# Making the one-hots of an edge sort column by column with scalars per partition, and loading the destinations first

## The chip, the cores and the metric

One core of a Trainium2 chip runs the kernel. Its engines are TensorE (PE), VectorE (DVE), ScalarE (ACT), GpSimd (POOL) and SyncE (SP); each works off its own list of instructions in order and waits on semaphores for the others. The metric is the device time of one execution in microseconds; less is better.

## What is computed

Four layers of a graph network on 1250 nodes with 512 features and 21250 edges (20000 random ones in both directions and a loop at each node, ordered by destination): an attention layer with batch normalization, an equivariant message layer, an attention layer followed by splines, and a mean aggregation. Each is followed by a residual addition and a layer normalization. Cut to what matters here:

```python
def reference(x, src, dst, edge_attr_4, edge_attr_8, ...):
    edge_index = stack([src, dst])
    x = layernorm(x + gat(x, edge_index, ...))              # per edge: h[src], softmax over dst
    x = layernorm(x + messages(x, edge_attr_4, edge_attr_8, edge_index, ...))
    x = layernorm(x + spline_attention(x, edge_index, ...))
    x = layernorm(x + mean_of_neighbours(x, edge_index, ...))
    return x
```

The kernel turns the edge list into a dense matrix of counts (how many edges lead from each node to each other), with which the attention layers work. For that the edges have to be grouped by blocks of nodes first. This grouping, the sort, is what the change touches.

## The kernel before

**Layout of the edges.** The 21250 edges lie as 125 partitions x 170 columns (`EC` = 170). VectorE computes for each edge the place it has in an order by blocks (40 groups of destinations for the records, then 20 groups for the counts): one-hot masks, a scan along the free dimension, totals over the partitions by TensorE (lines 825 to 831), and from these a place, which is split into a tile (0 to 203) and a lane (0 to 127).

**The sort.** TensorE moves two values per edge, the source `src_f` and the destination within its block `dl1`, to their lane and tile: for each of the 170 columns one matmul with weights [125 edges x 128 lanes], which hold the value at the edge's lane, and moving data [125 edges x 204 tiles], a one-hot of the tile. All accumulate into two PSUM banks. The columns go in 17 rounds (`ROUNDS`) of 10 (`SB`), with buffers for 3 rounds (`SBUFS`). In a round VectorE makes the lane one-hots of ten columns in one `tensor_tensor` (line 1962), the tile one-hots in another (1963), and multiplies the lane one-hots by the source in a third (1965). Their operands are broadcast: `iota2` holds each number twice, and two columns lie interleaved. ScalarE makes the second product, lane one-hot times `dl1`, by one ACTIVATE Copy with a scale per partition for each column (`scale_lanes`, line 1468). TensorE waits for both (835, 839). Between the rounds VectorE clears a fifth of the count matrix in rounds 4 to 8 (1967) and adds the residual identity to `w_skip` in round 10 (1974).

**What runs beside it.** TensorE works off node blocks of the first layer (`gat_block`, line 856) before the rounds and after the fourth and ninth batch; ScalarE copies them out (`gat_out`, 1473). At the end of the rounds stand small products for the attention rows (862, 871) and the group numbers (902 to 929). GpSimd writes the 170 columns of edge records to DRAM, one indirect DMA each (line 728), from the moment that VectorE has their places (1906) until long after the sort; ScalarE reads them back (1555) for an MLP on TensorE (1011 to 1036).

**Behind the sort.** VectorE copies the sorted lists out of PSUM (1987, 1988), makes one-hots of them (1996, 2005), TensorE counts pairs (942), ScalarE evicts (1524), VectorE adds (2015). Then follow the mask (2029), the maxima over neighbours of eight heads (2050) and the attention heads (2080, 2084, 1638, 1090).

**The start.** SyncE issues, in this order, `dst`, `src`, the two edge attributes, the second half of `x` (lines 542 to 549, two DMAs each), then 16 small DMAs of attention vectors, the clearing of the records in DRAM and the small weights. ScalarE's queue begins with the first half of `x` and `w_gat` (1431 to 1433). VectorE's first real work (1859) waits for `dst`. TensorE's list begins with the totals that VectorE's first scan (1865) gives (825), then come the transposes of `x` (849).

Of the kernel before, what the change touches and what calls it, by code (L numbers as in the profile page):

```python
# [12 lines left out]
EC = E // NP  # L13
# [80 lines left out]
def build(nc, a, out):  # L94
# [8 lines left out]
    with ctx:  # L103
# [6 lines left out]
        def sem(name):  # L110
            return ctx.enter_context(nc.semaphore(name))
# [70 lines left out]
        def nxt(shape, dt=f32):  # L182
# [43 lines left out]
        tile_f, lane_f = dstf.bitcast(f16)[:, 0:EC], posf.bitcast(f16)[:, 0:EC]  # L226
        src_f = dstf.bitcast(f16)[:, EC:2 * EC]
# [3 lines left out]
        lane_oh, lane_src, lane_dl = (at(off, [NP, SBUFS * PR, 2 * 128], f16).rearrange("p a (c t) -> p a c t", t=2)  # L231
                                      for off in (9980, 1020, 2940))
        tile_oh = cnt_s[:].rearrange("p b n -> p (b n)")[:, 4 * N:4 * N + SBUFS * PR * 2 * NSORT].bitcast(f16)\
            .rearrange("p (a c t) -> p a c t", a=SBUFS * PR, t=2)
# [174 lines left out]
        s_lane_ok = sem("s_lane_ok")  # L409
        s_lane_cp = sem("s_lane_cp")  # L410
# [128 lines left out]
        def _(sp):  # L539

            x_rows = a["x"].rearrange("(b p) n -> p b n", p=NP)
            for dst_tile, view, done in (
                    (dsti, a["dst"].rearrange("(p e) -> p e", p=NP), s_dst_in),
                    (srci, a["src"].rearrange("(p e) -> p e", p=NP), s_rec_in),
                    (a4, a["edge_attr_4"].rearrange("(p e) k -> p e k", p=NP), s_rec_in),
                    (a8, a["edge_attr_8"].rearrange("(p e) k -> p e k", p=NP), s_rec_in),
                    (x_sb[:, HB:, :], x_rows[:, HB:, :], s_x_in1)):
                for r in ROWS:
                    sp.dma_start(dst_tile[r], view[r]).then_inc(done, 16)
# [264 lines left out]
        def _(pe):  # L814
# [18 lines left out]
            def sort_batch(j):  # L833
                pe.wait_ge(s_sort_ok, j + 1)
                pe.wait_ge(s_lane_cp, j + 1)
                for n in range(SB):
                    r, e = (j % SBUFS) * PR + n // 2, n % 2
                    for q, lane in enumerate((lane_src, lane_dl)):
                        ins = t.matmul(PS[:, q, 0:NSORT], lane[:, r, :, e], tile_oh[:, r, :, e],
                                       start=(j == 0 and n == 0), stop=(j == ROUNDS - 1 and n == SB - 1))  # L840
                ins.then_inc(s_order_ps, 1)
# [586 lines left out]
        def _(act):  # L1428
            A = nc.scalar.activation

            for r in ROWS:
                act.dma_start(x_sb[r, 0:HB, :], a["x"].rearrange("(b p) n -> p b n", p=NP)[r, 0:HB, :]).then_inc(s_x_in, 16)
# [29 lines left out]
            def scale_lanes(j):  # L1462
                act.wait_ge(s_lane_ok, j + 1)
                if j >= SBUFS:
                    act.wait_ge(s_order_ps, 3 + j - SBUFS)
                for n in range(SB):
                    r, e, c = (j % SBUFS) * PR + n // 2, n % 2, j * SB + n
                    ins = A(lane_dl[:, r, :, e], lane_oh[:, r, :, e], ACT.Copy, scale=dl1[:, c:c + 1])  # L1468
                ins.then_inc(s_lane_cp, 1)

            def gat_out(b):
                act.wait_ge(s_h_ps, b + 1)
                A(h_sb[:, b, :], PS[:NP, 6 + b % 2, :], ACT.Copy).then_inc(s_h_cp, 1)
# [30 lines left out]
            for j in range(ROUNDS):  # L1504
                scale_lanes(j)
                if j in (4, 9):
                    gat_out(NB - 2 + j // 9)
                if j == ROUNDS - 3:
                    quad_out(0, 2)
                    quad_out(1, 3)  # L1510
                if j == ROUNDS - 2:
                    quad_out(2, 2)
                if j == ROUNDS - 1:
                    rows_out(0)
                    rows_out(1)
# [332 lines left out]
        def _(dve):  # L1848
# [102 lines left out]
            for j in range(ROUNDS):  # L1951
                if j >= SBUFS:
                    dve.wait_ge(s_order_ps, 3 + j - SBUFS)
                rs = slice((j % SBUFS) * PR, (j % SBUFS + 1) * PR)

                def of_pairs(vals, width):
                    return vals[:, j * SB:(j + 1) * SB].rearrange("p (a t) -> p a t", t=2).unsqueeze(2)\
                        .to_broadcast([NP, PR, width, 2])

                def numbers(width):  # L1960
                    return iota2[:NP, 0:2 * width].rearrange("p (c t) -> p c t", t=2).unsqueeze(1).to_broadcast([NP, PR, width, 2])
                v.tensor_tensor(lane_oh[:, rs], numbers(128), of_pairs(lane_f, 128), ALU.is_equal).then_inc(s_lane_ok, 1)
                v.tensor_tensor(tile_oh[:, rs], numbers(NSORT), of_pairs(tile_f, NSORT), ALU.is_equal)
                dve.wait_ge(s_lane_ok, j + 1)
                v.tensor_tensor(lane_src[:, rs], lane_oh[:, rs], of_pairs(src_f, 128), ALU.mult).then_inc(s_sort_ok, 1)
                if 4 <= j < 9:
                    ins = v.memset(cnt_d[:, (j - 4) * 2 * SPAN:(j - 3) * 2 * SPAN], 0)
                    if j == 8:
                        ins.then_inc(s_const0, 1)
# [573 lines left out]
```

## Time and profile before

| | us |
|---|---|
| median of three runs | 1570.6 (1567.6 to 1571.47) |
| the profiled execution | 1571.28 |
| its span | 1569.8 |
| busy: TensorE, VectorE, ScalarE, GpSimd | 1370.8, 1353.6, 903.3, 479.7 |
| first work on `dst` (VectorE, line 1859) | starts at 8.47 |
| rounds of the sort on VectorE | 70.39 to 135.9 |
| batches of the sort on TensorE | 86.5 to 144.5 |
| sorted lists read by VectorE | from 146.7 |

The profile is of one execution. Times in it count from the start of its span. A line such as L1468 is a line of the kernel. The chain of waits follows the work that ended last back through what released it; a timeline lists instructions in order of time, and neighbours of one line are merged (x50). "idle before" is the time for which the engine stood still ahead of the instruction, with the engine and line that ended it.

### The profile page before, as it was taken

The page shows a single profiled execution, that of the slowest core. Times are in us where ns is not written, and L with a number is a line of the kernel's source. Part 1 is how long each engine was busy: PE and PEld are TensorE (multiplying, and loading weights), DVE is VectorE, ACT ScalarE, POOL GpSimd, SP SyncE. Part 2 cuts the span into 40 slices and gives each one's busy share as a digit, 9 for nine tenths or more (in the row PEclk, how much of TensorE's full clock was granted, in tenths as well). Part 3 has the DMA queues.
Part 4 walks back from the last instruction along what each step waited for, and adds up shares of the span by engine and source line. Part 5 has one row for each costly group of instructions (what it writes and reads, how often), then busy time and mean ns, then how long its engine had stood idle before and what let it go on. Part 6 is the DMA issues. An engine that isn't in the chain of part 4 may idle for free.

```text
span 1569.8 us, 25159 instructions
## 1 busy us (share of the span) xinstructions
PE 1370.8 (87%) x8237; PEld 884.0 (56%) x8237; DVE 1353.6 (86%) x2066; ACT 903.3 (58%) x1949; POOL 479.7 (31%) x488
## 2 busy tenths in 40 slices
PE   2877988738688878689999999978999999999998
PEld 1555444512333333476666666765667777776465
DVE  7965999999899999869999999887989989997244
ACT  1176555718555555568888888642258849772400
POOL 1688888840001101226666666200000000000000
PEclk9799999859699999789999999988999999999999
DMA  8001000026211121247666766500144435333401
GB/s 195 4 6 8 7 7 7 6 79 173 69 56 57 37 72 22 69 131 214 204 197 191 216 201 195 91 1 1 41 147 135 134 121 174 135 134 100 126 20 46
DMA packets 77815, 150.27 MB, mean 96 GB/s; under 512 B 14850, under 2 KB 33396, under 8 KB 77605
## 3 DMA queue, kind: packets, MB, share of 16 engines
q1 hardware_dynamic: 51395, 83.19, 16.5%
q0 software_dynamic: 23328, 59.50, 14.9%
q10 hardware_dynamic: 3010, 6.59, 1.5%
q8 instruction: 38, 0.62, 0.2%
q14 instruction: 44, 0.36, 0.1%
HBM read 116.13 MB, written 32.91 MB: 95 GB/s over the span
## 4 chain that ended last, share of the span: by engine, by line
PE 45%; DVE 29%; issue 16%; ACT 5%; DVEq 3%; DMA 1%; POOL 0%; SPq 0%; POOLq 0%; ACTq 0%
PE PS L1320 14%; DVE arena L2084 7%; DVE arena L2050 5%; PE PS L1272 4%; DVE arena L2246 4%; PE PS L1330 4%; DVE arena L2080 3%; PE PS L1405 3%; PE PS L942 3%; ACT arena L1468 2%; PE PS L1385 2%; PE PS L1395 2%; DVEq L2246 2%; DVE arena L2005 2%; PE PS L1301 1%
## 5 line engine op out<-in xcount | busy, mean ns | idle before, releaser
L728 POOL DMA_INDIRECT recs<-arena x170 | 238.6, 1404 | 90.9 <-issue 90.3
L1090 PE MATMUL PS<-arena 125*128 125x512 f32 (+1 forms) x480 | 190.5, 535 | 41.6 <-DVE arena L2084 41.6
L792 POOL DMA_INDIRECT arena<-xup,gidx x205 | 195.0, 951 | 101.4 <-issue 49.3
L1178 PEld LDWEIGHTS PS<-arena 128*32 128x32 f32 x3280 | 173.1, 109 | 86.4 <-ACT arena L1706 79.8
L1706 ACT ACTIVATE arena<-arena,gslot 128x32 f32<-128x32 f32 x820 | 186.2, 309 | 51.8 <-PE PS L1178 45.4
L1178 PE MATMUL PS<-arena 128*32 128x128 f32 (+1 forms) x3280 | 200.4, 304 | 4.7 <-DVE arena L2238 2.2
L2238 DVE TENSOR_TENSOR arena<-PS,arena 128x1536 f32<-128x1536 f32 (+1 forms) x103 | 179.3, 1740 | 0.0
L1090 PEld LDWEIGHTS PS<-arena 125*128 125x128 f32 x480 | 86.0, 191 | 146.2 <-issue 78.1
L1638 ACT ACTIVATE arena<-arena,c 125x1250 f32<-125x1250 f32 x80 | 106.7, 1336 | 97.3 <-DVE arena L2080 97.2
L1320 PE MATMUL PS<-arena,cnt_d 128*125 128x256 f32 x576 | 147.8, 379 | 0.0
L2080 DVE SCALAR_TENSOR_TENSOR arena<-arena,c 125x1250 f32<-125x1250 f32 (+1 forms) x100 | 138.1, 1384 | 11.0 <-ACT arena L1760 9.9
L805 POOL DMA_INDIRECT cnt_d<-cnt_rows,bidx_c x1 | 0.9, 947 | 462.0 <-DVE bvalid L2471 462.0
L1164 PE MATMUL PS<-arena 64*128 64x512 f32 x410 | 117.7, 649 | 0.0
L1320 PEld LDWEIGHTS PS<-arena,cnt_d 128*125 128x125 f32 x576 | 108.1, 188 | 16.2
L1320 PE MATMUL PS<-arena 128*125 128x256 f32 x432 | 116.8, 379 | 0.1
L2084 DVE SCALAR_TENSOR_TENSOR arena<-arena,cnt_s 125x1250 f32<-125x1250 f32 x80 | 116.4, 1456 | 0.0
L1524 ACT ACTIVATE arena<-PS 125x626 uint16<-125x626 f32 x102 | 69.4, 692 | 60.4 <-PE PS L942 59.6
L1320 PEld LDWEIGHTS PS<-arena 128*125 128x125 f32 x432 | 81.0, 188 | 26.6 <-issue 16.4
L942 PE MATMUL PS<-arena 128*125 128x512 bf16 (+1 forms) x408 | 73.5, 311 | 15.9 <-DVE arena L2005 15.5
L2246 DVE TENSOR_TENSOR arena<-PS,arena 128x256 f32 x205 | 85.1, 415 | 1.3 <-PE PS L1178 0.5
L2234 DVE TENSOR_TENSOR arena<-PS,arena 128x512 f32<-128x512 f32 (+1 forms) x103 | 70.9, 688 | 15.4 <-PE PS L1164 12.6
L942 PEld LDWEIGHTS PS<-arena 128*125 128x125 bf16 x408 | 44.5, 142 | 64.4 <-DVE arena L2005 40.6
(395 smaller groups left out, 2537.6 us busy)
## 6 DMA issues: line engine op xcount, KB each, us to landing
arena<-in_spline_wT SPq DMA_DIRECT2D x32, 512.0 KB, 4.0
t_rows<-arena SPq DMA_DIRECT2D x18, 512.0 KB, 5.0
arena<-t_rows SPq DMA_DIRECT2D x18, 512.0 KB, 4.5
arena<-uv_rows SPq DMA_DIRECT2D x14, 610.4 KB
arena<-h_rows SPq DMA_DIRECT2D x26, 256.0 KB
h_rows<-arena SPq DMA_DIRECT2D x24, 256.0 KB, 2.8
arena<-xup,gidx POOLq DMA_INDIRECT x205, 3.6
cnt_rows<-cnt_s SPq DMA_DIRECT2D x1, 2734.4 KB
```

What stands on the lines that cost most here:

```text
L728: pool.indirect_dma_start(out=recs, out_offset=bass.IndirectOffsetOnAxis(pos[:, c:c + 1], 0), in_=rec[:, c, :], in_offset=None).then_inc(s ...
L792: pool.indirect_dma_start(out=ring[:, m, :], out_offset=None, in_=xup, in_offset=bass.IndirectOffsetOnAxis(gidx[:, par, m:m + 1], 0))\
L942: ins = t.matmul(PS[:NP, 2 * (n % 3) + q, 0:n1 - n0], oh_dst[:, n % (2 * WP), :, e], oh_src[:, 2 * (n % WP) + e, n0:n1], start=(e == 0), s ...
L1090: ins = t.matmul(PS[:, 3 * par + q, 0:n1 - n0], hs[:, sblk, par * C:par * C + 2 * C], wt[:, sblk % WR, n0:n1], start=(sblk == 0), stop=(sb ...
L1164: t.matmul(PS[:, tpw_bank[(2 * k + q) % 4], :], h3[r, buf, k * 128:(k + 1) * 128], w_m4[r, :], start=True, stop=True, tile_position=(q * H ...
L1178: ins = t.matmul(PS[quad * DB:(quad + 1) * DB, bank, o0 * MUL:o0 * MUL + w], sel4[:, s, v * DB:(v + 1) * DB], prod[:, s, c0 * MUL:c1 * MUL ...
L1320: ins = t.matmul(PS[:NP, bank, c * HD:(c + 1) * HD], lhs, w_part(g, w), start=(s == 0 and m in ((0, 1, 3, 6) if j == 0 else (0, 1, 3))), s ...
L1706: ins = A(sel4[:, s, y * DB:(y + 1) * DB], eq4[:, m // 4, s * DB:(s + 1) * DB], ACT.Copy, scale=gslot[:, par, c + R_Y + y:c + R_Y + y + 1])
L2080: v.scalar_tensor_tensor(dst, U, cc, V, ALU.add, ALU.max).then_inc(ok, 1)
L2084: v.scalar_tensor_tensor(dst, e, 1.0, cm, ALU.min, ALU.mult).then_inc(ok, 1)
L2238: v.tensor_tensor(pr[:, :, :, 1:4, :], w[:, :, :, 1, :].unsqueeze(3).to_broadcast([128, n, 2, 3, MUL]), xg[:, :, 1:4, :].unsqueeze(2).to_b ...
L2246: v.tensor_tensor(d, PS[:, 2 + m % 4, 0:256], d, ALU.add).then_inc(s_gsum_ok, 1)
```

## The change

Three edits go together. (1) The lane and tile one-hots are made one column at a time by VectorE, with the edge's lane, tile and value as scalars per partition: `(iota == lane) * src`, `(iota == lane) * dl1` and `iota == tile`, three `tensor_scalar` instructions per column. ScalarE scales none, the semaphores for that go, and `lane_f`, `tile_f`, `src_f` become float32. The columns are no longer interleaved. (2) Clearing the count matrix goes from VectorE's rounds to ScalarE, as five copies with scale 0 once the first round is made. ScalarE's other copies keep their order behind that. (3) SyncE loads `dst` first and waits for it before it issues any other load; ScalarE waits for it too before it issues its first.

```diff
-        tile_f, lane_f = dstf.bitcast(f16)[:, 0:EC], posf.bitcast(f16)[:, 0:EC]
-        src_f = dstf.bitcast(f16)[:, EC:2 * EC]
+        lane_f, tile_f, src_f = (at(off, [NP, EC]) for off in (10240, 10410, 10580))
...
         def _(sp):
+            for r in ROWS:
+                sp.dma_start(dsti[r], a["dst"].rearrange("(p e) -> p e", p=NP)[r]).then_inc(s_dst_in, 16)
+            sp.wait_ge(s_dst_in, 32)
             for dst_tile, view, done in (
-                    (dsti, a["dst"].rearrange("(p e) -> p e", p=NP), s_dst_in),
...
             def sort_batch(j):
                 pe.wait_ge(s_sort_ok, j + 1)
-                pe.wait_ge(s_lane_cp, j + 1)
                 for n in range(SB):
-                    r, e = (j % SBUFS) * PR + n // 2, n % 2
+                    r = (j % SBUFS) * SB + n
                     for q, lane in enumerate((lane_src, lane_dl)):
-                        ins = t.matmul(PS[:, q, 0:NSORT], lane[:, r, :, e], tile_oh[:, r, :, e],
+                        ins = t.matmul(PS[:, q, 0:NSORT], lane[:, r, :], tile_oh[:, r, :],
...
+            act.wait_ge(s_dst_in, 32)
             for r in ROWS:
                 act.dma_start(x_sb[r, 0:HB, :], ...)
...
-            def scale_lanes(j):
-                act.wait_ge(s_lane_ok, j + 1)
-                if j >= SBUFS:
-                    act.wait_ge(s_order_ps, 3 + j - SBUFS)
-                for n in range(SB):
-                    r, e, c = (j % SBUFS) * PR + n // 2, n % 2, j * SB + n
-                    ins = A(lane_dl[:, r, :, e], lane_oh[:, r, :, e], ACT.Copy, scale=dl1[:, c:c + 1])
-                ins.then_inc(s_lane_cp, 1)
+            def clear_counts(j):
+                return A(cnt_d[:, j * 2 * SPAN:(j + 1) * 2 * SPAN], ones[:NP, 0:1].to_broadcast([NP, 2 * SPAN]), ACT.Copy, scale=0.0)
...
-            for j in range(ROUNDS):
-                scale_lanes(j)
-                if j in (4, 9):
-                    gat_out(NB - 2 + j // 9)
...
+            act.wait_ge(s_sort_ok, 1)
+            act.wait_ge(s_consts, 1)
+            for j in range(NB // 2):
+                ins = clear_counts(j)
+            ins.then_inc(s_const0, 1)
+            for b in range(NB - 2, NB):
+                gat_out(b)
+            for q in range(3):
+                quad_out(q, 2 + q % 2)
+            for q in range(2):
+                rows_out(q)
             rows_out(2)
...
             for j in range(ROUNDS):
                 if j >= SBUFS:
                     dve.wait_ge(s_order_ps, 3 + j - SBUFS)
-                v.tensor_tensor(lane_oh[:, rs], numbers(128), of_pairs(lane_f, 128), ALU.is_equal).then_inc(s_lane_ok, 1)
-                v.tensor_tensor(tile_oh[:, rs], numbers(NSORT), of_pairs(tile_f, NSORT), ALU.is_equal)
-                dve.wait_ge(s_lane_ok, j + 1)
-                v.tensor_tensor(lane_src[:, rs], lane_oh[:, rs], of_pairs(src_f, 128), ALU.mult).then_inc(s_sort_ok, 1)
-                if 4 <= j < 9:
-                    ins = v.memset(cnt_d[:, (j - 4) * 2 * SPAN:(j - 3) * 2 * SPAN], 0)
+                for n in range(SB):
+                    r, c = (j % SBUFS) * SB + n, j * SB + n
+                    lane, tile = lane_f[:, c:c + 1], tile_f[:, c:c + 1]
+                    v.tensor_scalar(lane_src[:, r, :], iota_src[:NP, 0:128], lane, src_f[:, c:c + 1], ALU.is_equal, ALU.mult)
+                    v.tensor_scalar(lane_dl[:, r, :], iota_src[:NP, 0:128], lane, dl1[:, c:c + 1], ALU.is_equal, ALU.mult)
+                    ins = v.tensor_scalar(tile_oh[:, r, :], iota_src[:NP, 0:NSORT], tile, None, ALU.is_equal)
+                ins.then_inc(s_sort_ok, 1)
```

## Rows read from the trace of the kernel before

**Rows 1.** Chain of waits, the sort; start us, us, engine, line, count

```profile
83.44 5.71 ACT arena L1468 x20
...
146.50 0.20 DVE gpk L1983
```

**Rows 2.** Timeline of the sort by engine; start us, us, engine, line, operation, idle before

```profile
119.22 14.76 ACT L1468 ACTIVATE arena<-arena 125x128 f16<-125x128 f16 x50
...
70.39 0.82 DVE L1962 TENSOR_TENSOR arena<-iota,arena 125x1280 f16<-125x1280 f16 x1
...
72.99 0.82 DVE L1962 TENSOR_TENSOR arena<-iota,arena 125x1280 f16<-125x1280 f16 x1
...
89.14 0.82 DVE L1962 TENSOR_TENSOR arena<-iota,arena 125x1280 f16<-125x1280 f16 x1 [10.86 <-PE PS L839]
...
142.54 2.00 PE L839 MATMUL PS<-cnt_s,arena 125*128 125x204 f16 x20
```

**Rows 3.** Groups of VectorE by line, 83 to 146; count, busy us, mean ns, idle

```profile
L1967 DVE MEMSET cnt_d<- 125x1252 uint32 x5 | 5.5, 1102 | 1.1 <-issue 1.1
...
L1974 DVE TENSOR_TENSOR arena<-arena,ident 128x128 f32<-128x128 f32 x4 | 0.9, 281 | 0.0
```

**Rows 4.** Chain of waits, the start

```profile
1.51 6.94 DMA arena<-in_dst
```

**Rows 5.** Timeline of the start and of the second totals

```profile
13.86 14.32 DVE L1865 TENSOR_TENSOR_SCAN cnt_d<-cnt_s 125x6800 f16<-125x6800 uint16 x1
...
58.34 0.61 PE L830 MATMUL PS<-arena,upper 125*125 125x20 f32 x2 [3.94 <-DVE arena L1924]
```

**Rows 6.** DMA issues; count, KB each, median us from issue to landing

```profile
as_rows<-arena SPq DMA_DIRECT2D x1, 78.1 KB, 2.2
...
arena<-in_L_gnn_W_gat ACTq DMA_DIRECT2D x1, 1024.0 KB, 17.2
```

**Rows 7.** Groups of VectorE by line, whole run, shapes apart

```profile
L2029 DVE TENSOR_SCALAR arena<-cnt_d 125x12500 bf16<-125x12500 uint16 x1 | 3.4, 3416 | 0.0
...
L1863 DVE TENSOR_SCALAR cnt_s<-arena 125x170 uint16<-125x170 f16 x40 | 4.6, 199 | 0.0
```

**Rows 8.** Timeline of VectorE instructions with scalars per partition; line 2005's durations

```profile
L2005 DVE TENSOR_SCALAR arena<-iota_src,srt_s x204: 367/381/765, 148.0 to 277.6; 128x626 bf16<-128x626 f16 x102
...
159.33 0.67 DVE L2005 TENSOR_SCALAR arena<-iota_src,srt_s 128x626 bf16<-128x626 f16 x2
...
662.30 0.55 DVE L2197 TENSOR_SCALAR x_sb<-x_sb,mv,rstd 125x512 f32<-125x512 f32 x1
...
662.76 0.68 DVE L2203 TENSOR_TENSOR x_sb<-x_sb,PS 125x512 f32<-125x512 f32 x1
```

**Rows 9.** Timeline of GpSimd's scatters and the VectorE work beside them

```profile
48.37 2.35 DVE L1919 TENSOR_SCALAR arena<-arena 125x170 uint16<-125x170 f16 x20
...
48.88 2.90 POOL L728 DMA_INDIRECT recs<-arena  x1 [0.31 <-issue]
...
147.64 1.53 POOL L728 DMA_INDIRECT recs<-arena  x1 [0.30 <-issue]
...
148.04 2.13 DVE L2005 TENSOR_SCALAR arena<-iota_src,srt_s 128x626 bf16<-128x626 f16 x6
...
161.30 1.05 DVE L2005 TENSOR_SCALAR arena<-iota_src,srt_s 128x626 bf16<-128x626 f16 x2
```

**Rows 10.** Single lines, whole run; duration ns min/median/max, first and last start us

```profile
L728 POOL DMA_INDIRECT recs<-arena x170: 1174/1231/6907, 47.2 to 336.2; - x170
...
L1540 ACT ACTIVATE arena<-cnt_d x10: 1228/1238/1247, 280.3 to 307.6; 125x1250 f32<-125x1250 uint16 x10
```

**Rows 11.** Timeline of TensorE where the records and the maxima meet

```profile
402.28 4.56 PE L1041 MATMUL PS<-ident,uv 125*125 125x125 f32 x20 [8.62 <-DVEq L2070]
```

**Rows 12.** Two stretches: us, busy of PE, PEld, DVE, ACT, POOL, clock, DMA, GB/s

```profile
83.00:146.00 63.00, 48.83 (x408) 37.08 (x408) 43.79 (x55) 54.40 (x179) 52.48 (x35) 0.95 0.09 6
...
280.00:338.00 58.00, 33.41 (x154) 23.75 (x152) 56.03 (x86) 25.29 (x40) 46.37 (x37) 0.73 0.15 28
```

More of the change, by code:

```diff
@@ L230, in build @@
         iota2 = sb("iota2", [128, 2 * NT], f16)
[L231 to L234, printed above, removed]
+        lane_src, lane_dl = (at(off, [NP, SBUFS * SB, 128], f16) for off in (1020, 2940))
+        tile_oh = cnt_s[:].rearrange("p b n -> p (b n)")[:, 4 * N:4 * N + SBUFS * SB * NSORT].bitcast(f16)\
+            .rearrange("p (a c) -> p a c", a=SBUFS * SB)
         srt_s, srt_d = sb("srt_s", [128, NSORT]), sb("srt_d", [128, NSORT], f16)
@@ L408, in build @@
         s_sort_ok = sem("s_sort_ok")
-        s_lane_ok = sem("s_lane_ok")
-        s_lane_cp = sem("s_lane_cp")
         s_wt_ps = sem("s_wt_ps")
@@ L1502, in rows_out @@
                 A(rows16[:, n0:n1], PS[:2 * H, 2 + q % 2, 0:n1 - n0], ACT.Copy).then_inc(s_rows_cp, 1)
-            for j in range(ROUNDS):
-                scale_lanes(j)
-                if j in (4, 9):
-                    gat_out(NB - 2 + j // 9)
[L1508 to L1515, printed above, removed]
+            act.wait_ge(s_sort_ok, 1)
[9 more added lines that the diff above has]
+                rows_out(q)
             rows_out(2)
@@ L1953, in _ @@
                     dve.wait_ge(s_order_ps, 3 + j - SBUFS)
[L1954 to L1961, printed above, removed]
-                v.tensor_tensor(lane_oh[:, rs], numbers(128), of_pairs(lane_f, 128), ALU.is_equal).then_inc(s_lane_ok, 1)
-                v.tensor_tensor(tile_oh[:, rs], numbers(NSORT), of_pairs(tile_f, NSORT), ALU.is_equal)
-                dve.wait_ge(s_lane_ok, j + 1)
-                v.tensor_tensor(lane_src[:, rs], lane_oh[:, rs], of_pairs(src_f, 128), ALU.mult).then_inc(s_sort_ok, 1)
-                if 4 <= j < 9:
-                    ins = v.memset(cnt_d[:, (j - 4) * 2 * SPAN:(j - 3) * 2 * SPAN], 0)
-                    if j == 8:
-                        ins.then_inc(s_const0, 1)
+                for n in range(SB):
[5 more added lines that the diff above has]
+                ins.then_inc(s_sort_ok, 1)
                 if j == 10:
```

## The prediction, made before the result was known

> **What bounds the kernel now.** I read the chain of waits first, over the stretch in which the edges are sorted. There the chain runs on ScalarE: 20 copies of line 1468 from 83.44, then further trains of the same line up to the last batch, and VectorE takes over at 146.50 [rows 1]. The timeline shows the pace: 50 copies in 14.76 us, 0.295 us each, so ten for a round take 2.95 us [rows 2]. VectorE's own part of a round is shorter: left alone it starts rounds at 70.39 and 72.99, 2.60 us apart, three wide instructions each [rows 2]. The third thing to see there is the order of starts. VectorE is ready at 70.39 and makes three rounds, then idles 10.86 us until 89.14, because TensorE still works off node blocks and ScalarE has to evict them before it scales [rows 2]. So the stage starts with TensorE and runs at ScalarE's pace.
>
> The start of the kernel reads differently. The chain begins with 6.94 us of waiting for `dst`, issued at 1.51 and landed at 8.45 [rows 4]. From there VectorE's scan (13.86 to 28.18, [rows 5]) and a second one feed the totals for which TensorE waits 3.94 us until 58.34 [rows 5], and behind that TensorE does the blocks that hold up the sort. So time saved on `dst` moves VectorE, TensorE and the sort together.
>
> **The change, part by part.** *Loading first.* SyncE issues two `dst` DMAs and waits for them; ScalarE waits for the same before it issues half of `x` and `W_gat`. A lone store of 78.1 KB took 2.2 us from issue to landing [rows 6]; the second `dst` DMA is issued at 1.51, so I estimate a landing at 3.9 and a gain of 8.45 - 3.9 = 4.5 us. The bounds are 0 (if its 13-row piece is slow by itself) and 5.3 (landing at 3.2). Queued behind the wait on SyncE stand src, both edge attributes, the other half of x, the attention vectors, the clearing of recs and the small weights, all 2 to 3 us later; on ScalarE x, W_gat and the table load, 3 us later. W_gat, third in its queue, landed 17.2 us after its issue [rows 6]; issued by 5.3, behind the wait and `x`, it lands by 22.5. Its use stands behind TensorE's first totals, that is behind the scan, which would end near 23.7. I price these at nothing; if that cover is gone they take back at most the 4.5 us.
>
> *The one-hots.* Per round three wide VectorE instructions go, and ten copies on ScalarE. In their place come thirty narrow ones: twenty of 128 columns with two [P, 1] scalars, ten of 204 columns with one. The trace has none of this size with pointers, so I build the price from columns, fixed part and pointers.
> Columns: 125x12500 took 3.416 us and 125x170 0.199 us, both 2-byte and without pointers: 0.261 ns a column [rows 7]. So 128 columns are 33 ns, 204 are 53, 626 are 163.
> No pointer: 40 of 170 columns kept VectorE busy 4.6 us, 115 ns apart; less 44 for the columns, 70 ns are fixed [rows 7].
> One pointer: line 2005 (iota in f16, a float32 scalar, 2-byte output, the same form) has two in 0.67 us, of which the last takes its median of 0.381, so they follow each other at 0.29; less 163, 129 ns are fixed [rows 8]. The pointer costs about 60.
> Two pointers: line 2197 starts at 662.30 and the next instruction at 662.76; 512 float32 columns at twice the column price are 267 ns, so 193 ns are fixed [rows 8].
> A round is then 20 x (33 + 193) + 10 x (53 + 129) = 4.52 + 1.82 = 6.34 us, and 17 rounds 107.8 us, where the copies set 2.95 a round. TensorE's 20 matmuls of a round take 2.0 us [rows 2] and are hidden.
>
> Weighed against a rule: the Trainium skill ("VectorE: DVE Perf Modes", The TRN2 errata) gives 58 cycles plus columns over the mode's rate; an estimate by it is about 94 and 114 ns, a round of 3.0 us. The rows without a pointer lie near that rule, the rows with pointers do not, and I follow those.
>
> *GpSimd beside it.* GpSimd issues 170 scatters from 47.2 to 336.2, one every 1.71 us, all through the sort [rows 10]. The rows show that they and narrow VectorE work hold each other up. At 161.30 two of line 2005 took 1.05 instead of 0.67 us: 0.38 lost to one scatter. In the train of six at 148.04 (2.13 us, where five steps of 0.29 and a last of 0.38 make 1.83) 0.3 was lost over two scatters [rows 9]. The other way round, twenty of line 1919 ran unhindered (2.35 us) and the scatter at 48.88 took 2.90 us, where the median is 1.231 [rows 9]. So a scatter costs the new rounds 0 to 0.38 us. I take 0.2, nearest to the train of six, as that is the same instruction. At one scatter in 1.7 us: 107.8 / (1 - 0.2/1.7) = 122 us; the bounds are 107.8 and, at 0.38 in 1.48 (1.18 and 0.30 of idle), 145.
>
> *Clearing the counts* goes from VectorE (five memsets, 5.5 us [rows 3]) to ScalarE: 2504 columns each, where 1250 take 1.238 [rows 10], so 5 x 2.5 = 12.4 us from about 79 to 91. The node block behind it on ScalarE is made by TensorE only after the fourth batch, near 66 + 4 x 7.2 = 95, so it costs nothing; uncovered it would cost 12.4. VectorE's 5.5 us lay beside ScalarE's pace and give nothing back.
>
> *The sum.* VectorE starts the rounds at 70.39 - 4.5 = 65.9, needs 122 us, and 1 us for the residual weights between rounds [rows 3]: done at 189. TensorE's three buffers never hold it up, since it reaches the first batch at about 79 (83.44 - 4.5, [rows 1]) and then needs 2 us for what takes VectorE 7. Behind the last round stand one batch, a row product and the group rows; before, that took from 142.54 to 146.50, 4.0 us [rows 2]. TensorE will be idle most of this stage, and in a stretch where it was busy 33.4 of 58 us the mean granted clock was 0.73, part of it at 1.2 GHz [rows 12]; I take 5 us. VectorE then reads the sorted lists at 194 to 195 instead of 146.5: 48 us later. What follows is a serial chain (counts, mask, maxima, heads) and keeps that. Only the record path runs beside it: the last scatter starts at 336.2 [rows 10], and TensorE had worked off what hangs on it 8.62 us before VectorE let it go on at 402.28 [rows 11]. With everything else 48 us later it has more room.
> The profiled execution took 1571.3 us (span 1569.8), 0.7 above the median of the runs: 1571.3 + 48 = 1619, and against the median 1619 as well within its spread. I forecast 1619 us.
>
> **The rivals.** *Pointers cost nothing in a train* (not slower). If the read of a scalar is hidden behind the instruction in front, the fixed part is 70 ns: 20 x 103 + 10 x 123 gives 3.3 us a round, VectorE is done by 123, and TensorE's own work of the stage, 48.8 us [rows 12] from 79 on, ends it near 128. The lists come 18 us earlier: 1553. For it speaks only that no row has pointers on so few columns; against it that line 2005's instructions follow each other without a wait and still pay 129. It decides at a round of (146.5 - 5 - 1 - 65.9)/17 = 4.4 us, a mean of 146 ns an instruction; I sum up 211. By the rule of the Trainium skill above, this is the result that comes out.
>
> *GpSimd starves.* As under line 1919, scatters may get nowhere while the trains run. Then the rounds take 107.8 us and the lists come 33 us late, but the scatters lose those 107.8 us, less the 4.5 by which they begin sooner: 103. Less the 8.62 of room the records are 95 us late: 1666. It decides once the scatters slip by more than the lists' delay and 8.62. Against it: the scatter that met the train of six took 1.53 us, 0.3 more than the median of 1.231 [rows 9, 10], not the 2 us of the train.
> [...]
>
> *Loading first brings nothing*, as `dst` needs its time anyhow: 4.5 us more, 1623, inside the range.
>
> **How the numbers follow.** The forecast case (pointers paid, scatters sharing) has 0.81; starving 0.10; free pointers 0.06; 0.03 for something between that ends near no change. From the bounds: the low end is gain 5.3, no loss to scatters and a tail of 4, so 65.1 + 107.8 + 1 + 4 = 178, 31 late: 1602. The high end is 145 us and a tail of 7: 219, 72 late: 1644. Rounded, 1600 to 1645; what lies outside is free pointers, starving and the rest, 0.19. A measurement of this kernel tells 0.3% (about 5 us) from no change: faster 0.07, within 0.02, slower 0.91.
>
> **What would show it.** Right: line 1468 gone; the rounds' instructions 180 to 230 ns apart, some 0.2 to 0.4 more at a scatter; TensorE waiting for VectorE in the batches; VectorE's first idle ending near 3.9; the sorted lists near 194. Wrong: a mean under 146 ns per instruction, a `dst` landing after 6, scatters of many us in the sort with TensorE waiting for records past 440, or 2-byte columns at 128 wide that take more than 0.261 ns each, which would add 1 us a round.

## The result, and the profile after

The changed kernel takes 1622.8 us in the median (1620.7 to 1624.2), the kernel before 1569.1 in the runs beside it: a ratio of 1.0343, 95% interval 1.0325 to 1.0360. The profiled execution took 1624.2 us, with a span of 1622.7. The forecast was 1619.

VectorE turns to the sorted lists 52.0 us later: line 1965 at 198.52 stands where line 1983 stood at 146.50 before [rows 1]. ("The lists come at" means the start of this line in all that follows.) From there to the end of the span it takes 1622.7 - 198.5 = 1424.2 us, before 1569.8 - 146.5 = 1423.3. So all of the loss lies in the sort and in front of it, and the serial chain behind carries it to the end unchanged.

The timeline of the sort on TensorE and VectorE (start us, us, engine, line, operation; idle before and what ended it), against rows 1 and 2:

```profile
90.40 3.58 PE L836 MATMUL PS<-cnt_s,arena 125*128 125x204 f16 x20 [5.46 <-DVE cnt_s L1950]
97.80 3.58 PE L836 MATMUL PS<-cnt_s,arena 125*128 125x204 f16 x20 [3.82 <-DVE cnt_s L1950]
...
194.64 1.93 PE L836 MATMUL PS<-cnt_s,arena 125*128 125x204 f16 x20 [2.03 <-DVE cnt_s L1950]
...
198.52 0.20 DVE L1965 TENSOR_SCALAR gpk<-PS 1x52 int32<-1x52 f32 x1 [3.12 <-PE PS L926]
```

Batches start 7.40 us apart, and ahead of each TensorE stands still for VectorE's last one-hot. ScalarE, which set the pace before, no longer does. The same stretch seen from VectorE and GpSimd, two columns of the round and the scatter (one of GpSimd's indirect DMAs) that falls into them:

```profile
89.45 0.30 DVE L1948 TENSOR_SCALAR arena<-iota_src,arena 125x128 f16<-125x128 f16 x1
89.67 0.62 DVE L1949 TENSOR_SCALAR arena<-iota_src,arena 125x128 f16<-125x128 f16 x1
89.90 0.45 DVE L1950 TENSOR_SCALAR cnt_s<-iota_src,arena 125x204 f16<-125x204 f16 x1
90.26 0.30 DVE L1948 TENSOR_SCALAR arena<-iota_src,arena 125x128 f16<-125x128 f16 x1
90.48 0.34 DVE L1949 TENSOR_SCALAR arena<-iota_src,arena 125x128 f16<-125x128 f16 x1
90.75 0.26 DVE L1950 TENSOR_SCALAR cnt_s<-iota_src,arena 125x204 f16<-125x204 f16 x1
90.93 0.30 DVE L1948 TENSOR_SCALAR arena<-iota_src,arena 125x128 f16<-125x128 f16 x1
...
89.12 1.17 POOL L726 DMA_INDIRECT recs<-arena  x1 [0.30 <-issue]
90.60 1.17 POOL L726 DMA_INDIRECT recs<-arena  x1 [0.30 <-issue]
```

From 89.45 to 90.93 two columns take 1.48 us. Undisturbed instructions start 0.22 us apart, behind one of 204 columns 0.18. The two that are under way as a scatter ends drag: line 1949 takes 0.62 instead of 0.30 and ends at 90.29, with the scatter; line 1950 takes 0.45 instead of 0.26. Scatters also come 1.48 us apart: one for every two columns, five for a round, and none that starts in the rounds takes longer than 1.19.

The start, which the change brings forward (against rows 4 and 5):

```profile
3.20 0.25 DVE L1850 TENSOR_SCALAR arena<-arena 125x170 int32<-125x170 int32 x1 [0.77 <-DMA arena<-in_dst]
3.31 1.22 POOL L705 IOTA iota_src<- 128x1250 f16 x1
3.36 1.26 DVE L1851 TENSOR_SCALAR arena<-arena 125x170 int32<-125x170 int32 x1
...
4.72 2.40 POOL L707 IOTA iota<- 128x416 f16 x1
...
4.95 6.82 DVE L1854 TENSOR_SCALAR cnt_s<-arena 125x170 uint16<-125x170 f16 x40
```

`dst` is there at 3.20, where VectorE began at 8.47 before: 5.27 us. But a narrow instruction that took 0.24 us before takes 1.26, as long as the iota beside it, and the forty masks take 6.82 us, where they took 4.62. The rounds start at 68.34 instead of 70.39: 2.05 us are left of 5.27.

Two more rows, ScalarE's clearing and TensorE where the maxima come in (against rows 11):

```profile
79.64 10.99 ACT L1461 ACTIVATE cnt_d<-ones 125x2504 uint16<-125x2504 f32 x5
...
454.45 4.56 PE L1038 MATMUL PS<-ident,uv 125*125 125x125 f32 x20 [8.71 <-DVEq L2052]
```

The clearing lies where ScalarE has nothing else to do, and TensorE waits 8.71 us for VectorE at the heads, as before: neither the clearing nor the records are on the path.

### The profile page after: what moved, and what is told of

Its sections match the earlier page's. It is cut to its first block, busy times and chain, and to the rows that moved or that the text cites. A ratio compares the mean times of both kernels' runs of the same rounds, so it can differ in the third digit from the quotient of the medians.

```text
span 1622.7 us, 25418 instructions
## 1 busy us (share of the span) xinstructions
PE 1386.5 (85%) x8237; PEld 891.7 (55%) x8237; DVE 1430.0 (88%) x2520; ACT 864.4 (53%) x1784; POOL 462.9 (29%) x488
## 4 chain that ended last, share of the span: by engine, by line
PE 48%; DVE 35%; issue 12%; ACT 2%; DVEq 2%; DMA 1%; POOL 0%; SPq 0%; POOLq 0%; ACTq 0%
PE PS L1317 13%; DVE arena L2066 7%; DVE arena L2032 5%; PE PS L1175 5%; DVE arena L1949 4%; PE PS L1269 4%; PE PS L1327 4%; DVE arena L2062 3%; PE PS L1402 3%; DVE arena L2228 3%; PE PS L1161 3%; PE PS L939 3%; DVE arena L1948 2%; PE PS L1382 2%; PE PS L1392 2%
## 5 line engine op out<-in xcount | busy, mean ns | idle before, releaser
L726 POOL DMA_INDIRECT recs<-arena x170 | 222.2, 1307 | 88.8 <-issue 88.2
L836 PE MATMUL PS<-cnt_s,arena 125*128 125x204 f16 x340 | 50.7, 330 | 53.8 <-DVE cnt_s L1950 53.8
```

What stands on the lines that cost most here:

```text
L726: pool.indirect_dma_start(out=recs, out_offset=bass.IndirectOffsetOnAxis(pos[:, c:c + 1], 0), in_=rec[:, c, :], in_offset=None).then_inc(s ...
```

## The experiments

Each kernel was timed against the kernel before; spans and rows are of its profiled execution. From the heads to the end they need between 1163.7 and 1169.5 us, so shifts of 2 us are read from the traces, not from the medians.

**Is the load order worth anything in the changed kernel?** The changed kernel with the loads of before (label loads_back):

```diff
-            for r in ROWS:
-                sp.dma_start(dsti[r], ...).then_inc(s_dst_in, 16)
-            sp.wait_ge(s_dst_in, 32)
             for dst_tile, view, done in (
+                    (dsti, a["dst"].rearrange("(p e) -> p e", p=NP), s_dst_in),
...
-            act.wait_ge(s_dst_in, 32)
```

> The changed kernel with its loads issued in the order of before. Theory: in the changed kernel `dst` lands 5.3 us earlier (VectorE starts on it at 3.20 instead of 8.47), but VectorE's first two lines (1.26 instead of 0.24 us, 6.82 instead of 4.62 us) then run beside GpSimd's iotas (3.31 to 7.1) and lose 3.2 us, so only 2.05 us reach the sort. Undone, the rounds start at 70.4 instead of 68.34, the two lines take 0.24 and 4.62 us again, and the time is 2 us longer: about 1625. Rival (the whole 5.3 us count): about 1628. Second rival (the load order is worth nothing at the end): 1623.

Measured: 1622.6 us, ratio 1.0347 (1.0325 to 1.0369), the lists at 200.08, 1.6 us later than in the changed kernel. So the trace is near the theory and the median at the second rival. The loss is there without the new load order; as the clearing isn't on the path, it lies in the one-hots.

**The load order alone**, in the kernel before (loads_only: the lines of the diff above, the other way round):

> The kernel before with the load order of the changed one and nothing else. Theory: 2 us faster than before, 1567, with VectorE's first lines slowed by the iotas as in the changed kernel, and the chain of the sort (node blocks, then ScalarE's copies) shifted by the same 2 us. Rival (the gain of 4.5 to 5.3 us arrives): 1564. Rival (nothing arrives, as the sort starts with TensorE): 1569.

Measured: 1568.3 against 1568.3 us, ratio 1.000 (0.9987 to 1.0012). The timeline shows the same collision as the changed kernel, and the lists come at 144.47, 2.0 us earlier than in [rows 1], which the median doesn't show:

```profile
3.31 1.18 POOL L709 IOTA iota_src<- 128x1250 f16 x1
3.32 1.28 DVE L1863 TENSOR_SCALAR arena<-arena 125x170 int32<-125x170 int32 x1
...
4.91 6.82 DVE L1866 TENSOR_SCALAR cnt_s<-arena 125x170 uint16<-125x170 f16 x40
```

**Do the iotas eat the gain?** GpSimd makes its constants only when VectorE has its masks, in the changed kernel (iotas_late) and, with the load order, in the kernel before (loads_iotas):

```diff
+            pool.wait_ge(s_dve_chain, 3)
             pool.iota(iota_src[:], ...)
```

> The changed kernel, but GpSimd makes its number tables only when VectorE has made its first masks. Theory (a GpSimd instruction that runs holds VectorE up for up to its whole length): VectorE's first two lines take 0.24 and 4.62 us, the rounds start near 65.1 and the time is 3.2 us shorter, 1619.5. Rival (the masks were slow because other loads arrived beside them): the lines stay at 1.26 and 6.82 us and the time at 1623.

Measured: 1618.6 us, ratio 1.0319 (1.0297 to 1.0341); lists at 194.53, 4.0 us earlier. The masks take 4.62 us again, and now the iotas wait:

```profile
3.31 0.24 DVE L1852 TENSOR_SCALAR arena<-arena 125x170 int32<-125x170 int32 x1
...
3.87 4.62 DVE L1855 TENSOR_SCALAR cnt_s<-arena 125x170 uint16<-125x170 f16 x40
...
8.57 1.18 POOL L706 IOTA iota_src<- 128x1250 f16 x1 [5.31 <-DVE cnt_s L1855]
```

The masks end at 8.49 instead of 11.77, 3.28 us earlier: that is all of the 3.2 us that had got lost between `dst` and the rounds. The other 0.7 us are won between the masks and the first round (64.33 instead of 68.34), and what wins them stays open. The same in the kernel before:

> The kernel before with the new load order and with GpSimd's number tables behind VectorE's first masks; the one-hots as before. Theory: the 2 us of the load order and the 3.2 us of the iotas both arrive, 5.2 us faster than before: 1564. Rival (the start of the sort is held by TensorE's node blocks and by x, not by VectorE): under 2 us.

Measured: 1565.0 us, ratio 0.998 (0.9967 to 0.9994), lists at 139.14, 7.4 us earlier than before. So loading `dst` first is a small gain by itself, 0.2% and just clear of no change, once nothing of GpSimd's stands beside what it brings forward. One scatter of 5.01 us shows here; it ends at 117.21, about 1 us after VectorE stopped to wait for TensorE (2.39 us, until 118.55):

```profile
112.20 5.01 POOL L731 DMA_INDIRECT recs<-arena  x1 [0.30 <-issue]
...
118.55 0.83 DVE L1966 TENSOR_TENSOR arena<-iota,arena 125x1280 f16<-125x1280 f16 x1 [2.39 <-PE PS L842]
```

**What do the scalars from memory cost?** Constants in place of all of them (no_pointers), or of the value alone (one_pointer); the data sorted are then of no use:

```diff
# no_pointers; one_pointer keeps lane and tile and replaces src_f, dl1 by 2.0, 3.0
-  v.tensor_scalar(lane_src[:, r, :], iota_src[:NP, 0:128], lane, src_f[:, c:c + 1], ALU.is_equal, ALU.mult)
-  v.tensor_scalar(lane_dl[:, r, :], iota_src[:NP, 0:128], lane, dl1[:, c:c + 1], ALU.is_equal, ALU.mult)
-  ins = v.tensor_scalar(tile_oh[:, r, :], iota_src[:NP, 0:NSORT], tile, None, ALU.is_equal)
+  v.tensor_scalar(lane_src[:, r, :], iota_src[:NP, 0:128], 5.0, 2.0, ALU.is_equal, ALU.mult)
+  v.tensor_scalar(lane_dl[:, r, :], iota_src[:NP, 0:128], 5.0, 3.0, ALU.is_equal, ALU.mult)
+  ins = v.tensor_scalar(tile_oh[:, r, :], iota_src[:NP, 0:NSORT], 7.0, None, ALU.is_equal)
```

> The changed kernel with constants in place of the scalars per partition (lane 5, values 2 and 3, tile 7): the same instructions on the same columns, no scalar read from memory. Its lists are of no use, the sort is left out in effect. Theory (each pointer costs 60 to 65 ns in a train): the three instructions follow each other at 103, 103 and 123 ns where no scatter is under way, a round takes 3.3 us or, if scatters cost 0.2 us each, up to 4; the sort is then bound by TensorE, the lists are read near 128 to 135 and the time is about 1555 to 1560. Rival (narrow instructions cost their 211 ns with or without pointers): 1623. Rival (scatters starve under a train of 100 ns instructions): scatters of several us in the sort.

Measured: 1573.8 us, ratio 1.003 (1.0003 to 1.0057), lists at 139.35. Instructions start 0.10 us apart, 0.12 behind one of 204 columns, as the theory has it. But the lists are later than it wants, and one scatter starves, as the second rival had it: it waits many times its usual 1.18 us and takes 20.94, while all others in the rounds stay under 1.3:

```profile
114.08 0.17 DVE L1948 TENSOR_SCALAR arena<-iota_src 125x128 f16<-125x128 f16 x1
114.17 0.18 DVE L1949 TENSOR_SCALAR arena<-iota_src 125x128 f16<-125x128 f16 x1
114.28 0.20 DVE L1950 TENSOR_SCALAR cnt_s<-iota_src 125x204 f16<-125x204 f16 x1
114.40 0.88 DVE L1956 TENSOR_TENSOR arena<-arena,ident 128x128 f32<-128x128 f32 x4
...
114.38 20.94 POOL L726 DMA_INDIRECT recs<-arena  x1 [0.30 <-issue]
```

It ends at 135.3, 0.4 us behind the last one-hot. The records are late for it: the last scatter starts at 347.6, and TensorE begins the heads at 406.97, although VectorE came to its last maximum at 392.9 (in the changed kernel at 452.6, 1.8 us ahead of the heads). That is why lists that come 7 us earlier than before end in a kernel that is not faster.

> The changed kernel with the edge's value replaced by a constant: every instruction has one scalar per partition. Left out: the sorted values. Theory: the 128-column instructions follow each other at 162 instead of 226 ns, a round takes 5.06 us without scatters; scatters then cost more each, since less pointer time hides them (0.28 us at one in 1.48 us), 6.2 us: the rounds end near 174 instead of 194.5 and the time is about 1602. Rival (the second pointer is free): 1623.

Measured: 1592.5 us, ratio 1.0152 (1.0136 to 1.0167), lists at 169.13. Steps are 0.16 us for 128 columns and 0.18 for 204. Here too one scatter starves, from 133.98 to 165.95, the end of the rounds. The eleven rounds before it take 5.91 us each (6.2 were expected), the six beside it 5.08; hence 1592 instead of 1602. Both times the starved scatter starts with the four additions of the residual weights (rows of one_pointer):

```profile
133.68 0.88 DVE L1956 TENSOR_TENSOR arena<-arena,ident 128x128 f32<-128x128 f32 x4
...
133.98 31.97 POOL L726 DMA_INDIRECT recs<-arena  x1 [0.30 <-issue]
...
169.13 0.20 DVE L1965 TENSOR_SCALAR gpk<-PS 1x52 int32<-1x52 f32 x1 [3.52 <-PE PS L926]
```

**What do the scatters cost?** In the changed kernel they wait for the end of the rounds (scatters_after):

```diff
+            pool.wait_ge(s_sort_ok, ROUNDS)
             for c in range(EC):
```

> The changed kernel, but GpSimd starts its 170 scatters only when the last round of one-hots is made. Theory: without scatters a round takes 6.34 us instead of 7.40 (0.21 us lost per scatter, five in a round), the rounds need 108.7 us with the residual weights and the lists are read 17 to 18 us earlier, at 181. The scatters then run from 177 to about 445, so the records come late: their MLP would start near 450 instead of 396, and the time is some 35 to 45 us longer than that of the changed kernel, about 1660 to 1668. Rival (scatters don't slow the rounds): a round stays at 7.4 us.

Measured: 1681.6 us, ratio 1.0717 (1.07 to 1.0733). The rounds without scatters, and the place where it is paid back:

```profile
149.78 3.40 PE L837 MATMUL PS<-cnt_s,arena 125*128 125x204 f16 x20 [2.71 <-DVE cnt_s L1951]
156.07 3.43 PE L837 MATMUL PS<-cnt_s,arena 125*128 125x204 f16 x20 [2.89 <-DVE cnt_s L1951]
...
178.84 0.20 DVE L1966 TENSOR_SCALAR gpk<-PS 1x52 int32<-1x52 f32 x1 [3.53 <-PE PS L927]
...
L1950 DVE TENSOR_SCALAR arena<-iota_src,arena x170: 296/300/307, 67.1 to 174.4; 125x128 f16<-125x128 f16 x170
...
514.10 2.12 PE L1039 MATMUL PS<-ident,uv 125*125 125x125 f32 x17
```

A round takes 6.29 us, no one-hot of line 1950 (1949 in the changed kernel, where it took up to 0.63 us) is longer than 307 ns, and the lists come 19.7 us earlier: 18.3 in the rounds and 1.4 in front of them, where scatters are missing too (the first round starts at 66.92 instead of 68.34). But the last scatter starts at 455.0, and the heads wait for its records until 514.1, though VectorE came to its last maximum at 489.6. The time was expected at 1660 to 1668, with the last scatter near 445: behind the sort the scatters come 279 / 169 = 1.65 us apart on average, beside the rounds 1.48. That accounts for 10 us of the miss.

**What starves a scatter?** one_pointer with the additions behind the last round (adds_behind):

```diff
                 if j == 10:
-                    dve.wait_ge(s_small_in, 16 * NSM)
-                    for k in range(KT):
-                        d = w_skip[:, k, k * 128:(k + 1) * 128]
-                        v.tensor_tensor(d, d, ident[:], ALU.add)
...
+            dve.wait_ge(s_small_in, 16 * NSM)
+            for k in range(KT):
+                d = w_skip[:, k, k * 128:(k + 1) * 128]
+                v.tensor_tensor(d, d, ident[:], ALU.add)
             dve.wait_ge(s_gc_cp, 1)
```

> one_pointer (src and dl1 replaced by constants, so the output is of no use) with the four additions of the residual weights moved from round 10 to behind the last round. Theory: the scatter that took 31.97 us in one_pointer began at 133.98, 0.30 us into these additions (133.68 to 134.56), and once it had lost against them the one-pointer trains behind never let it in. Without a tensor_tensor inside the rounds no scatter is starved: all scatters of the sort 1.2 us long, all 17 rounds at the 5.91 us of the first eleven (not the 5.08 of the starved ones), lists at 68.7 + 17 x 5.91 + 0.9 + 4 = 174, that is 5 us later than one_pointer's 169.1; last scatter near 323 instead of 353.9; time 1597 us. Rival: any one-pointer train starves a scatter sooner or later, the additions were chance: a scatter of 10 us or more again somewhere in the rounds, lists near 169, 1592 us.

Measured: no scatter of the sort longer than 1.19 us; at the place in question:

```profile
133.66 1.19 POOL L726 DMA_INDIRECT recs<-arena  x1 [0.31 <-issue]
135.15 1.18 POOL L726 DMA_INDIRECT recs<-arena  x1 [0.30 <-issue]
```

The lists come at 173.19 (174 expected), the last scatter starts at 322.7 (323 expected). The median of 1591.7 us, ratio 1.0138 (1.0114 to 1.0161), misses the 1597 expected: the lists are 4.1 us later than in one_pointer and the span 3.0 longer, but the medians of the two are equal within their spread. In one_pointer the additions did start the starving.

One_pointer with two scalars from memory in round 11 (round_of_two):

```diff
-  ... lane, 2.0, ALU.is_equal, ALU.mult)
+  ... lane, src_f[:, c:c + 1] if j == 11 else 2.0, ALU.is_equal, ALU.mult)
```

> one_pointer (constants for src and dl1; no use as output) with the additions where they were, but in round 11, the one behind them, the src one-hots take their second scalar from memory again. Theory: an instruction with two scalars from memory leaves a gap in which a waiting scatter gets in (in the changed kernel one began at 149.78, 0.34 us into the additions, and took 1.19 us). Then the scatter that begins near 134 ends within about 2 us, the rounds keep 5.91 us (6.5 for round 11), lists near 174, time 1597. Rival: a scatter that has lost once waits until VectorE is idle, whatever follows: some 31 us again, lists at 169.7, 1593 us.

Measured: 1591.7 us, ratio 1.0138 (1.0113 to 1.0163), lists at 170.20. Half of each:

```profile
133.31 0.88 DVE L1956 TENSOR_TENSOR arena<-arena,ident 128x128 f32<-128x128 f32 x4
...
133.62 2.21 POOL L726 DMA_INDIRECT recs<-arena  x1 [0.31 <-issue]
136.13 25.26 POOL L726 DMA_INDIRECT recs<-arena  x1 [0.30 <-issue]
```

The scatter that began in the additions got through in 2.21 us, as the theory wanted. The next one, at 136.13, began in round 11 itself, with no addition near, and starved for 25.26 us, 3.6 us of them beside two-scalar instructions. So the theory falls as it stood: two scalars from memory don't always let a scatter in, and an addition need not stand beside the scatter that starves. The rival falls as well. The scatter got in at 161.39 in the middle of the train, nearly 5 us before the rounds end at 166.26, and VectorE had not stopped; three one-hots drag as they do at any scatter, and the train goes on:

```profile
160.69 0.69 DVE L1948 TENSOR_SCALAR arena<-iota_src,arena 125x128 f16<-125x128 f16 x1
160.86 0.56 DVE L1949 TENSOR_SCALAR arena<-iota_src,arena 125x128 f16<-125x128 f16 x1
161.02 0.45 DVE L1950 TENSOR_SCALAR cnt_s<-iota_src,arena 125x204 f16<-125x204 f16 x1
161.39 0.24 DVE L1948 TENSOR_SCALAR arena<-iota_src,arena 125x128 f16<-125x128 f16 x1
```

The order of starts might decide. In the changed kernel 82 of the 86 scatters that start in the rounds do so 0.11 to 0.13 us behind a start of line 1949; each round trip of 1.48 us puts the next one at the same place, and all get through. The additions, or the longer scatter at 133.62, shift that place. But this isn't shown: in one_pointer scatters start at three places of a column and get through at each, and in the changed kernel a scatter that began 0.34 us into the same additions took 1.19 us. Which places lose stays open.

**One of ten columns scaled by VectorE.** From loads_iotas (one_column), as a middle way between the two kernels:

```diff
-                for n in range(SB):
+                for n in range(SB - 1):
                     ... ins = A(lane_dl[:, r, :, e], lane_oh[:, r, :, e], ACT.Copy, scale=dl1[:, c:c + 1])
...
+                r, c = (j % SBUFS) * PR + PR - 1, j * SB + SB - 1
+                v.tensor_scalar(lane_dl[:, r, :, 1], lane_oh[:, r, :, 1], dl1[:, c:c + 1], None, ALU.mult)
                 v.tensor_tensor(lane_src[:, rs], lane_oh[:, rs], ...)
```

> The kernel before with the new load order, the number tables behind the first masks, and one of the ten columns of a round scaled by VectorE instead of ScalarE. Theory: ScalarE's part of a round falls from 2.95 to 2.66 us, VectorE's rises from 2.60 to about 2.8; VectorE's rounds with a memset (3.85 us) don't gain. From 14 rounds at 0.2 us: 2 to 3 us under the kernel with the load order and tables alone, about 1561. Rival (the pace is set by TensorE's blocks and VectorE's memsets between the rounds): no difference, 1564.

Measured: 1577.6 us, ratio 1.0047 (1.0032 to 1.0062), lists at 139.77. Both sides missed:

```profile
105.07 2.77 ACT L1472 ACTIVATE arena<-arena 125x128 f16<-125x128 f16 x9 [1.27 <-DVE arena L1966]
109.11 2.78 ACT L1472 ACTIVATE arena<-arena 125x128 f16<-125x128 f16 x9 [1.27 <-DVE arena L1966]
...
116.09 16.62 POOL L731 DMA_INDIRECT recs<-arena  x1 [0.30 <-issue]
```

ScalarE's nine copies wait for VectorE, whose rounds with a clearing are now the longer ones, and another scatter starves, this time beside the wide instructions. The records come late (heads at 407.48, maxima at 393.8). The scatter in front of it, at 114.36, began in the additions (113.86 to 114.75). This holds for all five kernels with a scatter of 5 us or more in the sort: it is the scatter that starts with the additions, or the next one. The same with the clearings in the 10 us in which VectorE waits for TensorE (clears_early):

```diff
-                if 4 <= j < 9:
-                    ins = v.memset(cnt_d[:, (j - 4) * 2 * SPAN:(j - 3) * 2 * SPAN], 0)
-                    if j == 8:
-                        ins.then_inc(s_const0, 1)
+                if j == SBUFS - 1:
+                    for i in range(5):
+                        ins = v.memset(cnt_d[:, i * 2 * SPAN:(i + 1) * 2 * SPAN], 0)
+                    ins.then_inc(s_const0, 1)
```

> one_column with the five clearings of the counts moved from rounds 4 to 8 to behind round 2, into the 10 us in which VectorE waits for TensorE. Theory: one_column gained nothing because its VectorE rounds with a clearing last longer than ScalarE's nine copies (two waits of 1.27 us on VectorE in ScalarE's rows) and because VectorE, without a pause, starved a scatter for 16.6 us, which made the records late. With the clearings out of the way VectorE keeps its lead of three rounds and pauses each round: no scatter over 3 us behind the first three rounds, the waits of ScalarE for VectorE gone, lists near 137 (one_column 139.8), records not late, 1562 to 1564 us. Rival: VectorE's rounds of 2.8 us plus what scatters take still leave no pause, a scatter starves again for over 10 us, records late, 1573 to 1578 us.

Measured: 1562.8 us, ratio 0.9951 (0.9931 to 0.9970), lists at 137.70. ScalarE's copies run without a wait for VectorE, and the longest scatter behind the first three rounds takes 2.61 us:

```profile
111.88 13.30 ACT L1472 ACTIVATE arena<-arena 125x128 f16<-125x128 f16 x45
...
110.69 2.61 POOL L731 DMA_INDIRECT recs<-arena  x1 [0.30 <-issue]
...
393.19 2.45 PE L1044 MATMUL PS<-ident,uv 125*125 125x125 f32 x20
```

The records are no longer early, though: the heads start 2.87 us behind the last maximum (390.32), where 1.83 are usual, since TensorE works at the records until then. This is the lowest median of the study, 60 us under the change as it was made, but not clearly ahead of loads_iotas: the intervals of the two touch, and the heads start only 0.7 us earlier than there (393.88).

## Why the prediction was right

**The round, confirmed.** 6.34 us were summed up from columns, a fixed part and some 60 ns for each scalar; without scatters it measured 6.29. (For one scalar the sum has 129 ns fixed, where its rows give 0.67 - 0.381 us less 163 ns, 126: 0.03 us in a round.) The three step sizes behind it hold singly: 0.10, 0.16 and 0.22 us for 128 columns with no, one and two scalars from memory, where the sum has 0.103, 0.162 and 0.226. The rule of the Trainium skill ("VectorE: DVE Perf Modes", The TRN2 errata) that the prediction weighed, by its estimate some 94 ns an instruction, lies near the step without scalars and near no other.

**The scatters, one of two sizes off.** The 0.2 us for each held: (7.40 - 6.29) / 5 = 0.22. But the sum put them 1.7 us apart, the mean over all of before [rows 10], and kept 1.48 (1.18 and the gap of 0.30) for its upper bound; 1.48 is what a scatter and its gap take where nothing holds it up, and in the rounds nothing did. By the prediction's own formula 1.48 gives 107.8 / (1 - 0.2/1.48) = 124.6 us instead of 122; with the additions 125.6, and 126.2 were measured (68.34 to 194.58), against 123 forecast.

**The start, the step that was mis-sized.** `dst` came 5.27 us earlier (4.5 forecast), but only 2.05 arrived at the rounds. The prediction named the queues behind the new wait, and not GpSimd's list, which VectorE now meets: its iotas, which had run before VectorE's first work, now run beside it and cost 1.0 us in line 1851 and 2.2 us in the masks. iotas_late gave 4.0 us back, 3.28 of them by the end of the masks. loads_only shows that this belongs to the load order, not to the one-hots.

**The tail** was 3.9 us, not 5. TensorE's granted clock in the rounds was as low as feared, 0.70 in the mean, so part of the time at 1.2 GHz (batches of 3.58 us in place of 2.00 [rows 2]), but the last batch took 1.93 us: the stretch of the rounds in the profile's windows (us, busy of PE, PEld, DVE, ACT, POOL, clock, DMA share, GB/s), to be read against rows 12:

```profile
65.00:190.00 125.00, 73.27 (x391) 50.23 (x391) 124.72 (x508) 15.65 (x14) 99.25 (x85) 0.70 0.11 7
```

Together: start +2.4, rounds +3.2, tail -1.1 make the lists 4.6 us later than the 193.9 of the sum, and the time 1622.8 instead of 1619. The shorter tail covers a part of what the start and the rounds cost more. VectorE's 124.72 us of 125 also say that it hardly ever waited for another engine there; what GpSimd costs it lies inside its instructions.

**The clearing** cost nothing, as forecast, with 10.99 us for 12.4. **The record path** had the room that was claimed: from the last scatter's start to the heads it needs 56 to 59 us (347.6 to 406.97, 351.3 to 407.48, 455.0 to 514.1), and the last scatter starts at 317.6, 137 us ahead of the heads at 454.45.

**The rivals.** *Free pointers* fell on its premise. It was also overpriced: with no scalar from memory at all the kernel took 1573.8 us and not 1553, with lists at 139.35 and not 128, and with records that came late because one scatter starved. *GpSimd starves* didn't happen in the changed kernel, but it is no phantom: single scatters of 16 to 32 us showed in four variants, and scatters_after, which holds all of them back, went to 1681.6. The prediction's argument against it (a scatter that met six narrow instructions and took 1.53 us) was too weak to exclude it. Why all 86 of the rounds got through isn't settled, so on this point the forecast was right by luck as much as by its argument. The Trainium skill ("SBUF — State Buffer", Who interferes with whom) has the first of the two block the other for its whole instruction, where VectorE runs in a 2-port perf mode. Line 1851 beside an iota fits that (1.26 us beside 1.22), though no trace shows its mode. The starved scatters don't: they wait through dozens of VectorE's instructions. Nor do the scatters that got through: VectorE lost 0.22 us to each, and not its 1.18. *Loading brings nothing* came near the truth for a reason it didn't have: the load was faster, and the gain was lost behind it.

## What to carry to other kernels

A per-partition scalar from memory costs VectorE some 60 ns an instruction here, so per-column one-hots with two of them are dearer (0.22 us for 128 columns) than a wide broadcast instruction plus ScalarE's copies beside it, even where the count of operations falls; sum up columns, fixed part and scalars from rows before moving work between engines. When a load or a wait moves forward, look also at what the other engines do in the time it moves into. And when VectorE is kept busy without a pause beside GpSimd's DMAs, watch the longest one: a single starved scatter can make a path late that had room. What starts the starving is known here in one case only (the additions in one_pointer).

## What the runs showed of the hardware that was not expected

- A GpSimd instruction held a narrow VectorE instruction up for as long as it ran: 0.24 us became 1.26 beside an iota of 1.22, and 3.86 in no_pointers, from 3.28 to 7.14, beside three of 1.18, 0.23 and 2.39 that end at 7.03.
- A scatter that loses against VectorE can wait through long trains of VectorE's instructions: 31.97, 25.26, 20.94 and 16.62 us, where its median is 1.18. Three of the four ended with the rounds, where VectorE paused; the one of 25.26 us got in without a pause. In one_pointer the rounds ran faster for it, 5.08 instead of 5.91 us.
- Two streams of different length fell into step: VectorE's columns of 0.63 us and GpSimd's scatters of 1.17 + 0.30 us locked at one scatter for two columns, and the same two instructions of the pair paid each time.
